# Graph layer and expert FFN on one core: fetched rows summed on chip and written plainly, fetches issued ahead of the last scatters, b2 kept on chip, small blanks, fetches that skip rows

## The reference, cut to what matters

```
x = x + relu( segment_sum( (layernorm(x) @ W)[src] * norm_src[src], dst ) * norm_dst + b )   # 6250 nodes, 106250 edges, 256 features
xn = layernorm(x)
logits = xn @ Wr + br;  top 2 of 8 experts per token, weights renormalised
y_e = gelu( (layernorm(xn) * ln_g[e] + ln_b[e]) @ W1[e] + b1[e] ) @ W2[e] + b2[e]            # 256 -> 1024 -> 256
x = x + sum over the two chosen experts of weight * y_e
```

## Time and profile before

| | us |
|---|---|
| median of 3 runs | 1616.14 (1612.79 to 1617.56) |
| the profiled execution, its own time | 1614.85 |
| its span in the trace | 1613.3 |
| PE, DVE, ACT, POOL busy | 1166.9, 1023.7, 644.5, 1153.6 |
| mean granted TensorE clock | 0.849 of full speed |

### The profile page before, as it was taken

How to read it: one execution, slowest core, us unless ns; L and a number is a source line. 1 busy time by engine, 2 the same in 40 slices (tenths; PEclk the granted TensorE clock), 3 DMA queues, 4 the chain that set the end, 5 groups by cost and what they waited for, 6 DMA issues and landing times. The chain is left out here.

```text
span 1613.3 us, 27172 instructions
## 1 busy us (share of the span) xinstructions
PE 1166.9 (72%) x9182; PEld 995.2 (62%) x9182; DVE 1023.7 (63%) x2809; ACT 644.5 (40%) x1273; POOL 1153.6 (72%) x1088
## 2 busy tenths in 40 slices
PE   6961756675661849879699696978949877899771
PEld 6961535463551738768578595856838665697661
DVE  8994757777683765847557475675746566666540
ACT  4964332124111424434245252424414353565550
POOL 8885777777777777777777777777777706786523
PEclk9999757666665979989899798988969998999996
DMA  8359878767757678777787777768668799999991
GB/s 255 114 177 340 295 257 274 255 208 246 236 190 249 193 247 276 233 258 251 224 289 249 254 251 251 245 222 264 218 208 264 241 280 270 264 324 295 308 304 21
DMA packets 271600, 395.38 MB, mean 245 GB/s; under 512 B 25205, under 2 KB 230935, under 8 KB 267365
## 3 DMA queue, kind: packets, MB, share of 16 engines
q1 hardware_dynamic: 205736, 244.70, 45.4%
q0 software_dynamic: 59360, 142.53, 29.8%
q10 hardware_dynamic: 6364, 6.40, 1.3%
HBM read 309.00 MB, written 85.67 MB: 245 GB/s over the span
## 5 line engine op out<-in xcount | busy, mean ns | idle before, releaser
L920 POOL DMA_INDIRECT gt<-zt,srcI x768 | 786.4, 1024 | 242.2 <-issue 177.9
L1325 PE MATMUL ps<-gt,S 128*128 128x257 f16 x1536 | 295.2, 317 | 172.1 <-DMA gt<-zt,srcI 161.6
L1443 PE MATMUL ps<-xe,w1b 128*128 128x256 f16 (+1 forms) x2736 | 336.3, 278 | 27.5 <-DVE xe L1901 16.9
L1272 ACT ACTIVATE h<-ps,cb 128x256 f32<-128x256 f32 (+1 forms) x456 | 224.5, 543 | 289.4 <-PE ps L1443 280.5
L1325 PEld LDWEIGHTS ps<-gt,S 128*128 128x128 f16 x1536 | 190.7, 151 | 231.6 <-DMA gt<-zt,srcI 207.0
L1458 PE MATMUL ps<-w2b,hT 128*128 128x256 f16 x2544 | 305.2, 278 | 16.8 <-DVE yb L1935 9.0
L1443 PEld LDWEIGHTS ps<-xe,w1b 128*128 128x128 f16 x2736 | 264.5, 103 | 70.4 <-DVE xe L1901 20.9
L1458 PEld LDWEIGHTS ps<-w2b,hT 128*128 128x128 f16 x2544 | 252.8, 100 | 52.5 <-issue 15.9
L1908 DVE SCALAR_TENSOR_TENSOR hT<-h,cb,hT 128x512 f16<-128x512 f32 (+1 forms) x228 | 161.3, 711 | 145.8 <-ACT hT L1276 145.2
L1276 ACT ACTIVATE hT<-h,cb 128x512 f16<-128x512 f32 (+1 forms) x228 | 157.8, 692 | 7.4
L951 POOL DMA_INDIRECT xs<-xrow,slI x98 | 100.8, 1029 | 77.2 <-DMA xs<-blank 47.6
(11 more groups left out here) (292 smaller groups left out, 1510.8 us busy)
## 6 DMA issues: line engine op xcount, KB each, us to landing
w1b<-ws SPq DMA_DIRECT2D x57, 1024.0 KB, 7.2
w2b<-ws SPq DMA_DIRECT2D x57, 1024.0 KB
ws<-w2b SPq DMA_DIRECT2D x16, 1024.0 KB, 5.2
xb<-xs SPq DMA_DIRECT2D x49, 260.0 KB, 7.6
gt<-zt,srcI POOLq DMA_INDIRECT x768, 4.7
ys<-yb SPq DMA_DIRECT2D x34, 256.0 KB, 5.0
zg<-zf SPq DMA_DIRECT2D x8, 1028.0 KB
gt<-zg SPq DMA_DIRECT2D x8, 1028.0 KB, 9.7
```

What stands on the lines that cost most here:

```text
L920: e.indirect_dma_start(out=gt[:, i % NG, :], out_offset=None, in_=zt, in_offset=bass.IndirectOffsetOnAxis(ap=srcI[:, c, r:r + 1].bitcast(u ...
L1272: inst = e.activation(h32[n % NH][:, z, 0:w], UP[n % 2][:, z * BS:z * BS + w], ACT.Gelu, bias=cb[m % 3][:, 2 * q + z:2 * q + z + 1], scale ...
L1325: inst = e.matmul(PS[r % 2][:, 0:257], S[:, r % NS, :, c], gt[:, i % NG, part * 257:part * 257 + 257], start=(c == 0 and part == 0), stop= ...
L1443: inst = e.matmul(UP[n % 2][:, z * BS:z * BS + 128 * size(m)], w[:, l, kk, j * 128:(j + 1) * 128], xe[m % 2][:, k, kk, 0:128 * size(m)], s ...
```

## The change

- `cc` becomes two `scalar_tensor_tensor`, the first with `row(t)` as its second input, so that `row(t)` holds the node's own row plus both experts' parts. `nd2` no longer writes the tiles 0 to 40 to `out`. The four `sums` are plain writes, and they no longer wait for one another or for gives.
- In `plan()` gives are listed only when all four sums are, and the first give waits for all of them. `cg` may be listed ahead of the last chunk's scatters (8 of the 41 are), `cc` only after `r5` of the last chunk, and a fetch is taken to land 4.0 us after its issue instead of 2.0.
- The block of zeros in `ys` is gone. Fetches have a bounds check, so that a row that isn't stored is skipped and its buffer keeps what it held. Its weight is set to zero by one more instruction in `r9`.
- The blanks are 128 rows (`HS`) behind each expert's last row, listed after the last chunk's scatters. The wait for them moves from POOL's scatter to SP's first load of rows of the last chunk.
- All of b2 is loaded once (1 MB, replicated) at the start of SP's program, and `y` takes its expert's row from it by a register. The load of 128 KB for each block and its semaphore are gone.

In the new order of steps: `cg` 0 to 7 stand behind the last gather and `st` 33; `cc` 0 stands ahead of the last chunk's scatters, `cc` 1 behind `r7`; the sums stand behind `cg` 17, 23, 33 and 40; the first give stands behind the last sum and all 23 gives follow it; `cc` 40 stands between `up` 3 of block 43 and the first `up` of block 44.

```diff
@@ plan()
-    yield [[("xs", ...) ...] + [("sent", c, ())],
-           [("r6", ...), ("regs", c, ())] + ([("r7", ...)] if c == LAST else [])
+    yield [[("xs", ...) ...] + [("sent", c, ())],
+           [("blanks", ex, ()) for ex in range(E if c == LAST else 0)], [("r6", ...), ("regs", c, ())] + ([("r7", ...)] if c == LAST else [])
...
-    if c == LAST - 1:
-        yield [[("blanks", ex, ()) for ex in range(E)]]
...
-        if max(s["chain"], s["base"]) > s["now"] or clock["POOL"] > s["now"] + 2.6 or LAST not in sent:
+        if clock["POOL"] > s["now"] + 2.6:
...
-            emit("sums", b, (("POOL", 1.3 * (SUMS[b][1] - SUMS[b][0])),), s["now"])
+            emit("sums", batches.popleft()[1], (("POOL", 2.0),), s["now"])
...
-        elif gives and (BLOCKS[gives[0]][0] < LAST or s["late"] <= s["now"]):
+        elif gives and s["summed"] == NSUM and s["chain"] <= s["now"] and (BLOCKS[gives[0]][0] < LAST or s["late"] <= s["now"]):
...
-                if kind == "cg" and (clock["POOL"] > s["now"] + 2.5 or LAST not in sent):
+                if kind == "cg" and (clock["POOL"] > s["now"] + 2.5 or LAST not in sent and arg >= NC - 2):
+                    continue
+                if kind == "cc" and s["placed"] <= LAST:
                     continue
@@ pool()
                 if last is None:
-                    e.wait_ge(s_base, 16 * BASE_DMAS)
                     e.wait_ge(s_out, 16 * OUT_DMAS)
-                elif last[0] == "give":
-                    e.wait_ge(s_give[last[1] % 2], given(last[1]))
+                    for b in range(NSUM):
+                        e.wait_ge(s_sums[b], 16)
                 else:
-                    e.wait_ge(s_sums[last[1]], 16)
+                    e.wait_ge(s_give[last % 2], given(last))
...
-                    if c == LAST:
-                        e.wait_ge(s_blank, 16 * (E + 1))
...
-                            in_offset=bass.IndirectOffsetOnAxis(ap=cidx[:, i, t:t + 1].bitcast(u32), axis=0)
-                        ).then_inc(s_cg[t % NC], 16)
+                            in_offset=bass.IndirectOffsetOnAxis(ap=cidx[:, i, t:t + 1].bitcast(u32), axis=0),
+                            bounds_check=last_stored, oob_is_err=False).then_inc(s_cg[t % NC], 16)
...
                     e.wait_ge(s_comb, b1)
-                    wait_last()
-                    last = ("sums", arg)
-                    e.dma_start(out=out[...], in_=acc[:, b0:b1, 0:256], accum_op=ALU.add).then_inc(s_sums[arg], 16)
+                    e.dma_start(out=out[...], in_=acc[:, b0:b1, 0:256]).then_inc(s_sums[arg], 16)
@@ sync()
+            e.dma_start(b2all[:, :, :].rearrange("p e d -> p (e d)"), b2.rearrange("e d -> (e d)").partition_broadcast(128)).then_inc(s_misc, 16)
...
-                    if full > a0:
+                    if full > a0 >= TG:
...
-                    e.dma_start(xs[bass.ds(at, FRESH), :].rearrange("(n p) c -> p n c", p=128), ...
+                    e.dma_start(xs[bass.ds(at, HS), :].rearrange("(n p) c -> p n c", p=128), ...
...
                             for z in range(NSC):
                                 e.wait_ge(s_sc[z], sent(c, z))
+                            if c == LAST:
+                                e.wait_ge(s_blank, 16 * (E + 1))
...
-                    if m >= 2:
-                        e.wait_ge(s_yread, m - 1)
-                    e.dma_start(b2b[m % 2][:, :], b2[bass.ds(regs[m][0], 1), :].to_broadcast([128, D])).then_inc(s_b2[m % 2], 16)
@@ vector()
+                        then(e.scalar_tensor_tensor(out=wts[:, :, 0:TG], in0=pidx[:, :, :], scalar=float(M0 * BS), in1=wts[:, :, 0:TG],
+                                                    op0=ALU.is_lt, op1=ALU.mult))
...
-                                           scalar=cb[m % 3][:, 10:11], in1=b2b[m % 2][:, :].unsqueeze(1).to_broadcast([128, n, D]),
+                                           scalar=cb[m % 3][:, 10:11], in1=b2all[:, bass.ds(expert[m], 1), :].to_broadcast([128, n, D]),
...
-                    if t == 0:
-                        e.wait_ge(s_base, 16 * BASE_DMAS)
-                    then(e.tensor_scalar(row(t), fetched_rows(t, 0), wts[:, 0, t:t + 1], None, ALU.mult))
+                    then(e.scalar_tensor_tensor(out=row(t), in0=fetched_rows(t, 0), scalar=wts[:, 0, t:t + 1], in1=row(t),
+                                                op0=ALU.mult, op1=ALU.add))
```

More of the change, by code:

```diff
@@ L45 @@
 LAST = len(CHUNKS) - 1
-FRESH = -(-(N - CHUNKS[LAST][0] * 128 + BS - 1) // 128) * 128
 MT = 10
-MB = max(NBLK)
+MK = max(NBLK[:-1] + [WHOLE, HALVES])
 OFF = [MT - (t1 - t0) if c == LAST - 1 else 0 for c, (t0, t1) in enumerate(CHUNKS)]
@@ L171, in send_stages @@
     yield [[("xs", (c, j), (("POOL", 2.56),)) for j in range(CHUNKS[c][1] - CHUNKS[c][0])] + [("sent", c, ())],
-           [("r6", c, (("DVE", 6.5),)), ("regs", c, ())] + ([("r7", c, (("DVE", 4.5),))] if c == LAST else [])
+           [("blanks", ex, ()) for ex in range(E if c == LAST else 0)], [("r6", c, (("DVE", 6.5),)), ("regs", c, ())] + ([("r7", c, (("DVE", 4.5),))] if c == LAST else [])
            + ([("r9", c, (("DVE", 2.0 + 0.13 * CHUNKS[c][1]),))] if c <= EARLY else [])]
     yield [[("routed", c, ())]]
-    if c == LAST - 1:
-        yield [[("blanks", ex, ()) for ex in range(E)]]
 PARTS = {"wa": ("w", "wb"), "wc": ("w", "wd"), "we": ("w", "wf"), "nW": ("n", "hh"), "r3": ("r", "r5")}
@@ L192, in plan @@
     clock = {"PE": 0.0, "DVE": 0.0, "ACT": 0.0, "POOL": 0.0}
-    s = {"now": 0.0, "bank": 0.0, "held": {}, "free": {}, "norms": -1, "nT": 0, "nW": 0, "hh": 0, "xr": 0, "placed": 0, "tabled": 0, "read": -1, "routed": -1, "loaded": 0, "asked": False, "given": 0, "base": 1e9, "late": 1e9, "summed": 0, "chain": 0.0,
+    s = {"now": 0.0, "bank": 0.0, "held": {}, "free": {}, "norms": -1, "nT": 0, "nW": 0, "hh": 0, "xr": 0, "placed": 0, "tabled": 0, "read": -1, "routed": -1, "loaded": 0, "asked": False, "given": 0, "late": 1e9, "summed": 0, "chain": 0.0,
          "pb": 0, "pe": 0, "pG": 0, "ps": 0, "pz": 0, "ph": 0, "po": 0, "pw": 0, "wj": 0, "zl": 0, "zat": 1e9}
@@ L422, in step_job @@
                     batches.append((end, [b1 - 1 for b0, b1 in SUMS].index(arg)))
-                if kind == "nd2" and ends(arg) in (LAST - 1, LAST):
-                    s["base" if ends(arg) < LAST else "late"] = end + 4.0
+                if kind == "nd2" and ends(arg) == LAST:
+                    s["late"] = end + 4.0
                 if kind == "sent":
@@ L428, in step_job @@
                     s["routed"] = arg
-                chain.at = end + 2.0 if kind == "cg" else s["now"] + 4.0 if kind in ("pl", "pw", "blanks") else s["now"] if kind == "xs" else end
+                chain.at = end + 4.0 if kind == "cg" else s["now"] + 4.0 if kind in ("pl", "pw") else s["now"] + 1.5 if kind == "blanks" else s["now"] if kind == "xs" else end
                 job.at = max(job.at, end)
@@ L528, in gnn_ffn @@
         xs = dram("xs", ((SPARE + 1) * BS, XW), f32)
-        ys = dram("ys", ((M0 + 1) * BS, D), f32)
+        ys = dram("ys", (M0 * BS, D), f32)
         ws = [dram(f"ws{i}", (E, 8, 128, 512), f16) for i in range(2)]
@@ L557, in gnn_ffn @@
         gone = sb("gone", [128, E], f32)
-        kio = sb("kio", [128, MB], f32)
+        kio = sb("kio", [128, MK], f32)
         pio = sb("pio", [128, 1], f32)
@@ L567, in gnn_ffn @@
         gdone = sb("gdone", [1, 1], f32)
-        zero = sb("zero", [128, 257], f32)
-        blank = sb("blank", [128, XW], f32)
+        spare = sb("spare", [128, XW + 1], f32)
+        zero, blank = spare[:, 0:257], spare[:, 1:XW + 1]
+        b2all = sb("b2all", [128, E, D], f32)
         PS = [ctx.enter_context(nc.psum_tensor(f"ps{i}", [128, 512], f32)) for i in range(8)]
@@ L637, in gnn_ffn @@
         e8j = sb("e8j", [128, E], i32)
[L638 to L641, removed]
+        kc = sb("kc", [128, MK, E], f32)
+        kd = sb("kd", [128, MK, E], f32)
+        kf = sb("kf", [128, MK], f32)
+        kr = sb("kr", [128, MK], f32)
         ek = [sb(f"ek{c}", [128, 2, max(n, 1)], i32) for c, n in enumerate(NBLK)]
@@ L659, in gnn_ffn @@
         pre.close()
-        b2b = [sb(f"b2b{i}", [128, D], f32) for i in range(2)]
         cb = [sb(f"cb{i}", [128, 12], f32) for i in range(3)]
@@ L695, in row @@
             return acc[:, t, 0:256]
-        CONST = ["ident0", "ident", "irep", "ones", "oneb", "pio", "tri", "area", "room", "gone", "rev", "kio", "tok", "mask0", "mask", "far", "zero", "blank0", "blank"]
+        CONST = ["ident0", "ident", "irep", "ones", "oneb", "pio", "tri", "area", "room", "gone", "rev", "kio", "tok", "mask0", "mask", "far", "blank0", "blank"]
         const = {n: i + 1 for i, n in enumerate(CONST)}
@@ L739, in gnn_ffn @@
         s_pst = [s_misc, s_const]
-        PST0 = [16 * 7, len(CONST)]
+        PST0 = [16 * 8, len(CONST)]
         s_pset = sem("s_pset")
@@ L802, in gnn_ffn @@
         XS_BEFORE = [sum(2 * (t1 - t0) for t0, t1 in CHUNKS[:c]) for c in range(len(CHUNKS) + 1)]
```

(23 more changed lines are left out.)

19 lines of the change are left out of this document (5 added, 14 removed).

## The result

The changed kernel took 1630.36 us in the median of 4 runs (1627.36 to 1631.71), the kernel before 1616.85 in 4 (1612.79 to 1617.63). The ratio is 1.0089, with a 95% interval of 1.0077 to 1.0102: 13.5 us slower, clear of noise. The forecast was 1613 with a range of 1594 to 1632, and 0.33 for slower. The time lies inside the range, but the kernel became 0.9% slower where the forecast had it 3 us faster. The profiled execution took 1627.36, its span is 1625.9.

What follows compares the result with a forecast made beforehand. POOL was taken to bound the kernel until 1290 us, then its chain of sums and gives: first give 1454.5, fifteen full gives 120 us to 1574.5, plus 36.7 and 1.55, makes 1612.8; forecast 1613, range 1594 to 1632.

Steps and rivals of the forecast that it cites:

- 0.33 for slower: Whole kernel: chance of ending slower, counted with the slow gives, clogged vector queue and void cases.
- The mechanism and its first half: POOL after the last gather: fetches, then the last sum's landing, set the first give at 1454.5.
- terms of -2.7, +1.7 and +1.0 us: Before the first give: last sum issued at 1445.5, landing in 10 us, one microsecond off for b2, base writes, skipped rows.
- 47.6 us of waiting for blanks: POOL, 1288.7 to 1336.3: scatters start only 3 us earlier without it; its worth is the eight fetch pairs fitting there.
- The last plain sum: Before the first give: the 1408 KB sum lands in 10 us as a plain write, against 18.7 as an accumulate.
- I take 7.4 for eight gives (59 us): From 1454.5 to about 1515, beside full blocks: each of eight full gives takes 7.4 us.
- seven gives at 8.7, 61 us: Last seven full gives, beside half blocks with DMA share 0.99: 8.7 us each.
- the tail 36.7: From the start of give 49: eight half gives and their last landing take 36.7 us.
- slow gives: Rival, last sum to give 48: gives meet weight loads all the way, 9.3 us each, ending at 1632; chance 0.20.
- the ring: Late blocks, within slow gives: `y` of block m waits for the give of m-8, so loads and gives come in step.
- The quick gives: Rival: alone in POOL's queue, full gives take 7.2 us or less, first at 1450, ending at 1596; chance 0.22.
- The quiet full give: Chain of gives, without other traffic: 1.9 us of issue plus 4.2 of a half give, 6.1.

Runs made afterwards that it cites:

- x4_blanks_b: Kernel before with only the blanks changed (128 rows, after the last scatters, wait on SP): 1616.57 us beside 1617.38, ratio 1.0004.
- x8_hyb_no_ahead_b: x3_hybrid_c with no fetch listed ahead of the last scatters: 1618.78 us beside 1617.38 for the kernel before, ratio 1.0018.
- x3_hybrid_c: Changed kernel without its plain sums: base rows, accumulating sums and gives among the fetches as before; 1611.70 us beside 1617.38 for the kernel before, ratio 0.9972.
- x9_thin_full: Changed kernel with weight loads of blocks 44 to 48 alone cut to one eighth: 1619.15 us when the kernel before took 1617.86.
- x2_plain: Changed kernel with gives as plain indirect writes, without the addition to out: 7.19 us for a full give, 2.98 for a half one.

## Why the prediction was wrong

**The mechanism and its first half were right.** POOL's queue and the last sum set the first give; it came at 1454.49 for 1454.5, but that the two agree so closely is luck, since terms of -2.7, +1.7 and +1.0 us cancelled. That 47.6 us of waiting for blanks were worth no more than what POOL can do in them is confirmed (`x4_blanks_b`: ratio 1.0004, 0.9989 to 1.0019), and so is it that the fetches in the gap are the gain (7.1 us between `x8_hyb_no_ahead_b` and `x3_hybrid_c`). b2 on chip, skipped rows and small blanks together, without fetches ahead, are no gain: 1.0018. The last plain sum: 10 forecast, 10.8 landed.

**The step that failed** is "I take 7.4 for eight gives (59 us)". They took 1527.80 - 1454.49 = 73.3 us, 9.2 each; the six of them that met loads took 10.0. The other terms: seven gives at 8.7, 61 us, measured 60.0; the tail 36.7, measured 38.1 (1587.79 to 1625.9). 14.3 - 1.0 + 1.4 = 14.7, and 1612.8 + 14.7 = 1627.5, the profiled 1627.36. A single term of the sum was mis-sized, and it carries the sign. That the seven came out is partly luck too: none took 8.7, five took 9.66 each beside loads and the last two 6.4 and 5.3 without. The blocks came later with the gives: `y` of block 45 ran at 1490.5 (1484 forecast) and the last `y` at 1588.0 (1576).

Why it was: the 7.4 rested on full blocks taking 11.3 us of TensorE each, and on no fetches sharing the software queue. The share was indeed lower, 0.84 against 1.08 later, but the gives there took 9.8, 10.6 and 9.7 against 10.4 and 10.5. An average share doesn't say what a give meets. SP issues the 2 MB of a full block within 3 us (1474.32 and 1476.80), as soon as buffers are free, and eleven of the fifteen gives have such a burst beside them. Where no load was issued (in the stall ahead of `y` 45 and behind the last load), or the loads beside it were thinned to an eighth, a give took 5.3 to 7.3. `x9_thin_full` shows it for this very term: with the loads of the full blocks thinned, the first three gives went from 9.8, 10.6 and 9.7 to 6.5, 7.3 and 6.8. The forecast had this rival, slow gives at 9.3 with the loads and gives in step, at 0.20. Its pitch was a little high (8.89 measured, as four of the fifteen met no load), its cause only partly right: taking the ring away saves 5.5 us of the chain, thinning the loads 35 (15 x 2.33).

**The quick gives** at 7.2 and less did not come. The rule that speaks for them, that each DMA engine takes its queues in turn (the Trainium skill, "DMA: Bandwidth & Descriptors", Queues, rings and completion order), is not refuted, but no short landing followed from it here: with the gives alone in POOL's queue, the weight loads of SP's queue still cost a full give 2.3 us on average.

**The quiet full give** I put at 6.1; it is 6.5.

**What the change traded.** Before, eleven full gives were issued with fetches behind them, where POOL had work while they landed; the twelfth, at 1518.92, stood behind the last fetch, and three stood alone behind the last sum. After, all fifteen stand alone: the chain from 1454.49 to 1587.79 replaces one whose last part ran from 1548.55. The plain sums took four landings of 12 to 19 us out of the chain, but had to come ahead of all gives. `x3_hybrid` keeps the overlap and the early fetches, and is the only version that was faster than the kernel before by more than the noise.

Not tried: the early fetches alone in the kernel before, with nothing else changed; gives of blocks of one expert, which share no token, without a wait between them; and weight loads held back while a give lands.

## What to carry to other kernels

A chain of small DMAs that must wait for one another is priced by what else is issued beside each, not by the average load of its stage; look for single landings with and without a burst beside them in the trace, and count how many of the chain's links will meet one. Before taking the longest wait away, look up the second thing that the waiting instruction needs: here it was ready only 3 us earlier. And making links cheaper by putting them all ahead of, or behind, the work that hid them can cost more than they did.

## What the runs showed of the hardware that was not expected

An accumulating indirect DMA is issued in 1.55 us on POOL, a plain one in 0.98 (`x2_plain`), and half gives come at 4.1 and 2.98 us. The quickest issue of a fetch with a bounds check takes 1.00 us instead of 0.94; the 82 fetches kept POOL busy for 88.0 us instead of 84.1. A sum of 1280 KB landed in 12.4 to 15.2 us as an accumulate and in 10.3 to 10.8 as a plain write. And the kernel before took 1610 to 1623 us in some periods and 1801 to 1852 in others. The changed kernel, which was traced in both, had most of the difference ahead of its last gather, and its pitch of gives did not change (8.89 and 8.87).
